# A two-layer hybrid block on one core: the last experts call split into two halves, the decoder taken tile by tile, and a planner's numbers set anew

## The reference

```python
x = x + local_attention(layernorm(x))     # "A": 16 heads, 44 fixed offsets (0..40, 96, 128, 384)
x = x + experts(layernorm(x))             # "F"
x = x + causal_attention(layernorm(x))    # "B": 16 heads, full causal softmax
x = x + experts(layernorm(x))             # "F" again, same weights

def experts(n):                                      # D=256, H=512, M=64, E=8
    cont   = sigmoid(n @ enc_W + enc_b) @ s2c_W + s2c_b          # 512 -> 64
    gates  = top2(softmax(tanh(cont @ rW1 + rb1) @ rW2 + rb2))   # renormalised
    h      = relu(cont @ We1[e] + be1[e])                        # 8 experts, 256 wide
    out    = sum_e gates[e] * (h[e] @ We2[e] + be2[e])
    spikes = sigmoid(out @ c2s_W + c2s_b)
    return layernorm(sigmoid(spikes @ dec_W + dec_b)) * ln_g + ln_b
```

## Time and profile before

| what | value |
|---|---|
| median of three timed runs | 1737.67 us (1734.58, 1737.67, 1738.28) |
| the profiled execution: its time | 1734.03 us |
| its span, first to last instruction | 1731.9 us |
| mean granted TensorE clock | 0.977 of full speed |
| busy: PE, DVE, ACT, POOL | 91%, 74%, 45%, 8% of the span |
| PE idle in front of a matmul, from 1655 us on | 14.2 us, in ten places |
| from the last decoder product to the end of the span | 11.5 us |

### The profile page before, as it was taken

The page is one execution under the profiler, slowest core; times in us unless marked ns, Lnnn a source line. Parts: engine busy times, 40 slices in busy tenths (PEclk is TensorE's granted clock), DMA queues, the critical chain, the costliest instruction groups (busy, mean ns, idle before and its releaser), DMA issues. The chain is left out here.

```text
span 1731.9 us, 28223 instructions
## 1 busy us (share of the span) xinstructions
PE 1580.9 (91%) x10560; PEld 882.0 (51%) x10560; DVE 1282.0 (74%) x3138; ACT 787.8 (45%) x1474; POOL 141.6 (8%) x155
## 2 busy tenths in 40 slices
PE   6599899999999999999999999999989998997976
PEld 2164465546555465554654556454655546454533
DVE  7969757896569966798767976699666996746633
ACT  1134346445364544644355353644536444552633
POOL 1010110101101020000101011010200001000000
PEclk9899999999999999999999999999999999998989
DMA  9230440014301161022500244001520216013000
GB/s 318 79 121 1 159 148 2 16 73 172 86 3 39 50 219 40 2 87 86 172 2 15 75 141 117 2 16 74 184 75 3 74 50 207 5 39 111 3 13 13
DMA packets 50261, 133.96 MB, mean 77 GB/s; under 512 B 6256, under 2 KB 22576, under 8 KB 45520
## 3 DMA queue, kind: packets, MB, share of 16 engines
q1 hardware_dynamic: 50128, 132.16, 23.3%
HBM read 80.99 MB, written 46.04 MB: 73 GB/s over the span
## 5 line engine op out<-in xcount | busy, mean ns | idle before, releaser
L1306 DVE TENSOR_TENSOR arena_AB<-qT,kT 128x2048 f32<-128x2048 f32 (+3 forms) x240 | 400.1, 1719 | 11.9 <-PE bank L1625 5.5
L1361 DVE CUSTOM_DVE_ANT_0 bank<-bank,causal_b 128x512 f32<-128x512 f32 (+3 forms) x512 | 234.1, 525 | 105.4 <-PE bank L1697 104.9
L1543 PE MATMUL bank<-arena_F,kept 128*128 128x512 f32 x512 | 235.6, 609 | 7.2 <-DVE arena_F L1451 4.8
L1625 PE MATMUL bank<-arena_AB,slot_w 128*32 128x512 f32 x1408 | 198.1, 612 | 32.6 <-DVE arena_AB L1306 31.4
L1135 ACT ACTIVATE arena_AB<-bank 128x512 f32<-128x512 f32 (+1 forms) x352 | 167.0, 585 | 70.2 <-PE bank L1713 69.8
L1168 ACT ACTIVATE arena_F<-bank,kept 128x512 f32<-128x512 f32 x256 | 159.0, 688 | 20.0 <-PE bank L1543 17.7
L1543 PEld LDWEIGHTS bank<-arena_F,kept 128*128 128x128 f32 x512 | 96.5, 195 | 124.7 <-issue 113.1
L1543 PE MATMUL bank<-cont_hi,by_cont 128*128 128x512 f32 (+1 forms) x272 | 115.9, 426 | 9.6 <-DVE arena_AB L1361 6.5
L1821 PE MATMUL bank<-kept,arena_F 128*128 128x256 f32 x512 | 117.0, 382 | 7.1 <-ACT arena_F L1185 6.6
L1543 PE MATMUL bank<-xnT,kept 128*128 128x512 f32 x256 | 120.0, 622 | 2.2 <-ACT xnT L1060 1.5
L1806 PE MATMUL bank<-arena_F,kept 128*64 128x512 f32 x512 | 120.5, 602 | 0.4 <-ACT arena_F L1181 0.2
(11 more groups left out here) (186 smaller groups left out, 2359.9 us busy)
## 6 DMA issues: line engine op xcount, KB each, us to landing
arena_AB<-band SPq DMA_DIRECT2D x32, 1344.0 KB, 6.6
arena_AB<-stacks SPq DMA_DIRECT2D x64, 384.0 KB
stacks<-arena_AB SPq DMA_DIRECT2D x48, 256.0 KB, 2.6
band<-arena_AB SPq DMA_DIRECT2D x32, 328.0 KB, 3.9
stacks<-xnT SPq DMA_DIRECT2D x32, 256.0 KB, 2.6
band<-kT SPq DMA_DIRECT2D x4, 1352.0 KB, 23.1
stacks<-xn SPq DMA_DIRECT2D x16, 256.0 KB, 3.0
kept<-kept_pack SPq DMA_DIRECT2D x1, 3765.0 KB, 18.8
```

Of the source, the lines that this page charges most:

```text
L1306: ins = nc.vector.tensor_tensor(prod[SET_AT[i]][:, col:col + c, :], qT[:, hf, :].unsqueeze(1).broadcast_to([P, c, T]), k, ALU.mult)
L1361: ins = nc.vector.tensor_tensor_reduce(out=s, in0=s, in1=causal[:, (TT - 1 - i) * P:T], scale=-1.0, scalar=BIG, op0=ALU.add, op1=ALU.min, ...
L1543: ins = nc.tensor.matmul(out(ps), w, x, start=n == 0, stop=n == len(pairs) - 1)
L1625: ins = nc.tensor.matmul(ps[HS * col:HS * (col + 1), :], slot_w[:, slot(n), :], prod[SET_AT[i]][:, col, :], start=r == 0, stop=False, skip ...
```

## The change

1. `calls()` replaces the last F call by two, stages `G` (tiles 0 and 1) and `H` (tiles 2 and 3). All code of an F call takes its tiles from `tiles_of(u)`, so that every product, read and copy of G and H has 256 columns in place of 512, and statistics and `close` run over two tiles. G waits for `pr` of tile 1 of the last attention call, H for `pr` of tile 3.
2. G and H have semaphores of their own. H has its own normalised rows, turned rows, `hid` ring and decoder output, in the part of memory that attention uses (`arena_AB`).
3. In all F calls, `dec` is four products of one tile each, a bank each, with one bias addition on DVE (`dec_b`, 256 columns) and one tanh each; the first step of the second statistics is `stat_2`, tile by tile.
4. In the planner: durations of a band's `write` and `read` by tile, `DEPTH` 1.55 to 1.95, and other offsets in `PULL` and `CALL_PULL`. These move steps in all calls.

```diff
+def tiles_of(u):
+    first = {"G": 0, "H": 2}.get(u.stage)
+    return range(TT) if first is None else range(first, first + 2)
@@ local_phases
-            p.put(("write", i), ("SP", 0.4, ("p", i, "ACT")), ("DMA", 2.6))
+            p.put(("write", i), ("SP", 0.4, ("p", i, "ACT")), ("DMA", (2.3, 2.3, 6.3, 5.0)[i]))
-                                        *([("pB", k - 2, 1, "PE")] if k >= 3 else [])), ("DMA", 7.0))
+                                        *([("pB", k - 2, 1, "PE")] if k >= 3 else [])), ("DMA", (6.6, 8.3, 6.0, 6.5)[k]))
@@ expert_phases
-    for n in range(TT // 2):
-        p.put(("dec", n), ("PE", 3.43, *[("c2s", m, "ACT") for m in range(KF)]), ("DVE", 0.61))
-        p.put(("tanh", n), ("ACT", 1.1, ("dec", n, "DVE")))
-    p.put("stats_2", ("DVE", 2.1, ("tanh", 0, "ACT"), ("tanh", 1, "ACT")))
+    for i in tiles:
+        p.put(("dec", i), ("PE", 1.72, *[("c2s", m, "ACT") for m in range(KF)]), ("DVE", 0.36))
+        p.put(("tanh", i), ("ACT", 0.5, ("dec", i, "DVE")))
+    for i in tiles:
+        p.put(("stat_2", i), ("DVE", 0.36, ("tanh", i, "ACT")))
+    p.put("stats_2", ("DVE", 0.6))
@@ calls
+    last = moe.pop()
+    moe.extend(Call(s, 0, last.batch, last.layer) for s in "GH")
@@ the tables, two lines of them
-TICK, DEPTH = 0.02, 1.55
+TICK, DEPTH = 0.02, 1.95
-    ("F", "PE"): {"turn": -620, "hid": 316, "eo": 1710, "dec": 10230},
+    ("F", "PE"): {"turn": 960, "rh": 479, "hid": 478, "eo": 2100, "dec": 9870},
@@ between_calls
-                needs.append((ATTENTION[n], ("pr", TT - 1), "DVE"))
+            needs.append((ATTENTION[min(n, len(ATTENTION) - 1)], ("pr", tiles_of(u)[-1]), "DVE"))
@@ build
+SIGNALS["G"] = SIGNALS["H"] = {**SIGNALS["F"], "xn_ready": 2, "dect_ready": 2}
+        hid_g = part(RH * T, at=STACKS).rearrange("p (r t) -> p r t", r=RH)
+        xn_g = part(TT * D, at=STACKS).rearrange("p (i c) -> p i c", i=TT)
+        xnT_g = part(KD * T).rearrange("p (k t) -> p k t", k=KD)
+        def rows_in(u):
+            return slice(tiles_of(u)[0], tiles_of(u)[-1] + 1)
+        def columns_in(u):
+            return slice(P * tiles_of(u)[0], P * (tiles_of(u)[-1] + 1))
@@ SP, experts
-                    sp.dma_start(rows_of(out_dram, u.batch), x_of[k][:]).then_inc(y_stored[k], 16)
+                    sp.dma_start(rows_of(out_dram, u.batch)[:, rows_in(u), :], x_of[k][:, rows_in(u), :]
+                                 ).then_inc(y_stored[k], 16)
@@ VectorE
-                    nc.vector.tensor_tensor(dd[:, 2 * p:2 * p + 2, :], ps[:].rearrange("p (i c) -> p i c", i=2),
-                                            c("dec_b").unsqueeze(1).broadcast_to([P, 2, D]), ALU.add
-                                            ).then_inc(read, 1)
+                    nc.vector.tensor_tensor(dd[:, p, :], ps[:, 0:D], c("dec_b"), ALU.add).then_inc(read, 1)
+                elif kind == "stat_2":
+                    dve.wait_ge(*nth(u, "dect_ready", p - tiles[0] + 1))
+                    tile_moments(u, dd, norm, p, "_2")
@@ TensorE
-                    product(u, name, lambda ps: ps[:], [(w, cont_hi), (w, cont_lo)])
+                    product(u, name, lambda ps: ps[:, 0:width], [(w, cont_hi[:, cols]), (w, cont_lo[:, cols])])
-                    for i in range(2):
-                        at = (2 * n + i) * P
-                        for k in range(KF):
-                            ins = nc.tensor.matmul(ps[:, i * D:(i + 1) * D], t_moe[:, k, at:at + P], dec_w[:, k, :],
+                    for k in range(KF):
+                        ins = nc.tensor.matmul(ps[:, 0:D], t_moe[:, k, n * P:(n + 1) * P], dec_w[:, k, :],
```

More of the change, by code:

```diff
@@ L125, in put, with norm_phases @@
             before = engine
-def norm_phases(p):
-    p.put("stats", ("DVE", 1.95))
+def norm_phases(p, tiles=TT):
+    p.put("stats", ("DVE", 0.6 + 0.34 * tiles))
     p.put("pow", ("POOL", 1.0, ("stats", "DVE")))
-    p.put("xn", ("DVE", 1.35, ("pow", "POOL")))
+    p.put("xn", ("DVE", 0.34 * tiles, ("pow", "POOL")))
     for k in range(KD):
-        p.put(("turn", k), ("PE", 0.44, ("xn", "DVE")), ("ACT", 0.48))
+        p.put(("turn", k), ("PE", 0.11 * tiles, ("xn", "DVE")), ("ACT", 0.16 + 0.08 * tiles))
 def output_phases(p, kind, i, on_needs, far):
@@ L305, in expert_phases @@
[L305 removed]
+        p.put(("c2s", m), ("PE", us(0.86, 0.0), ("eo", E // 2 - 1, "DVE")), ("ACT", us(0.6, 0.16)))
+    for i in tiles:
[4 more added lines that the diff above has]
+    p.put("stats_2", ("DVE", 0.6))
     p.put("pow_2", ("POOL", 1.0, ("stats_2", "DVE")))
[L307 removed]
@@ L308, in expert_phases @@
-    if layer == 1:
+    p.put("close", ("DVE", us(3.4, 0.2), ("pow_2", "POOL"), ("ln_b", "DVE")))
+    if u.layer == 1:
         p.put("store", ("SP", 0.4, ("close", "DVE")), ("DMA", 7.0))
@@ L1409, in gate_experts @@
+                link(u, nc.vector.tensor_tensor(same_, other, own, ALU.is_equal))
+                link(u, nc.vector.tensor_tensor(same_, same_, before, ALU.mult))
+                link(u, nc.vector.tensor_tensor(above_, above_, same_, ALU.add))
+                link(u, nc.vector.tensor_reduce(rank_, above_, AX, ALU.add))
+                link(u, nc.vector.tensor_scalar(rank_, rank_, 1.5, None, ALU.is_lt))
             def gate_experts(u):
+                rows, tiles = rows_in(u), len(tiles_of(u))
@@ L1471, in experts @@
                     link(u, ins)
-                    for i in range(TT):
+                    for i in tiles:
                         ins = nc.vector.scalar_tensor_tensor(
```

254 lines of the change are left out of this document (142 added, 112 removed), and 8 rows, old and new, of the table CALL_PULL.

## The result

The changed kernel takes 1730.23 us (median of five runs, 1728.38 to 1732.76), the kernel before 1737.67 (five runs beside it, 1734.58 to 1738.28): ratio 0.996, interval [0.9948, 0.9972]. It is faster, by 7.4 us or 0.4%; the forecast was 21.7. 1730 lies in the range of 1703 to 1733, near its slow end.

A forecast was written before the change was run, and what follows sets the result against it. PE, busy 91% of the span, was taken as the bound, its idle tenth all there is to win. 1734.03 - 12.8 (last call) - 1.7 (A1) - 2.7 (B6 into B7) - 1.5 (middle) = 1715.3, raised to 1716; range 1703 to 1733.

The forecast's parts named there:

- The band (place 3): Local attentions, third `pA`: less PE work covers tile 2's band read; 0.7 us lost in each of six calls, 4 lost.
- B7 beside the last but one experts call: Stretch from B6's last `pr` to B7's: other moves of `S`, `prod` and `hid` taken at nothing.
- The last call: Last experts call in halves G and H: entry, clock, inner waits and end, less the halves' cost; -12.8 us.
- Entry: Before G's `turn`: G needs only tiles 0 and 1, so PE's 5.61 us wait becomes 2.1; 3.5 gained.
- Clock: Behind the last call's entry: 3.9 us lost at granted clock 0.51, half of it regained; 1.9 gained.
- Inner waits: Last experts call: products of the other half fill five PE waits summing to 6.22 us; 5.8 gained.
- End: After PE's last product: chain to the last `close` 5.2 us against 8.0, plus 0.3 at the store.
- A1: Before A1's first `pA`: a decoder product moves behind tile 0's scores, so the band starts earlier; 1.7 us gained.
- B6 into B7: DVE does `on` 0 and 1 before most of B7's splits, ending PE's 3.01 us wait; 2.7 gained.
- End of a local attention (place 2): Behind B1 to B5's old-order waits of 0.89 and 1.33 us: new order gains 1.1 five times, 5.5.
- What would show it: Signs in the profile after, among them idle near 2 us before G's `turn` and near 1 at the third `pA`.
- The middle takes it all: Rival: end gains as forecast, new order loses 2 to 3 us per local attention; 1737, no difference; chance 0.08.

The follow-up runs named there:

- old_new_b6end_b7: old_new_b6end with F14 beside B7 also in the changed kernel's order, up to B7's `on`: 1721.41 us.
- old_order_halves: Order of the kernel before, decoder steps by tiles, up to B7's first `on`; from there the changed kernel's, with G and H: 1723.41 us, ratio 0.992.
- old_new_b6end: old_order_halves with B6's `on`, `oNT`, `pr` and B7's `lo` in the changed kernel's order: 1720.62 us, ratio 0.9903.

## Why the prediction was wrong

The forecast was for the profiled execution first, so its terms can be set against the marks of the two profiles, in us:

```
                                          before    after   change  forecast
start to the c2s beside A2                 405.6    405.7    +0.2    -1.7
from there to the c2s beside A7           1021.2   1026.0    +4.8    -2.2
from there to the last pr of B6            142.3    141.8    -0.5    -2.0
from there to the last pr of B7             95.7    102.3    +6.6     0
from there to the end of the span           67.1     53.8   -13.3   -12.8
```

- **The band (place 3): the step that failed.** It said "the read for tile 2 can start only after tile 0's `pA`", set PE's work from there against the landing, and took 0.7 us a call, 4 in all, since "part of it takes the place of small pauses after it". In the new order the read starts at the landing of its own write, 2.6 to 2.9 us later, since the scores now come later relative to `pA`. Measured are 3 us in each of six calls, 18 in place of 4: the waits for the band, 1.6 a call, took the place of no others (those of the stretch without them are 20.2 us, before 19.4), and the low clock behind them adds 1.1 a call. With the write ahead of one read 10.8 us of this came back. It could have been read ahead of time: the landing of that write in before, 5.8 to 8.4 us, set against the distance in the new order from its issue to the end of tile 0's `pA`, 5.2 to 5.6. A step whose place on its queue is unchanged moves all the same when what it waits for moves.
- **Luck in the same term.** The wait that it computed, 1.3 us at the median landing, is near the 1.6 measured, but by two errors. The cover it gave as 5.3 us was 7.6 to 8.1 in the six calls, and the read landed after 6.4 to 6.8. Had the read started with tile 0's `pA`, as I had it, there would have been no wait.
- **B7 beside the last but one experts call: put at nothing, 6.6 us in the profile.** "The moves of `S`, `prod` and `hid` otherwise I take at nothing" covers this stretch. Its order accounts for part: 4.3 us there on the old middle (old_new_b6end_b7), 3.0 of them given back behind. The eight profiles with this order and no fill in it have 102.3 us or more there, the six with the old one 98.5 or less; yet the median of that run moved by only 0.8, and how much stays in the time is open. Single executions of one kernel with the new middle lie up to 15 us apart.
- **The last call: right.** -12.8 forecast; -13.3 with the decoder by tiles (old_order_halves against before). Entry 3.5: idle 5.61 to 1.82, 3.8. Clock 1.9: 3.4 lost to 1.6, 1.8. Inner waits 5.8: 5.2. End 3.1: 2.65 on the chain and 0.8 at the store, 3.4. The four make 14.2, so the halves cost about 0.9 for 1.5. The pairs of 256 columns start 0.12 us apart, so two of them cost what one of 512 did; the doubt that a weight load might not hide is gone.
- **A1: the wait came out, the gain did not.** PE's idle time before the first band went from 5.74 to 4.10, 1.6 for 1.7. But that `pA` starts at 202.40 against 202.56, and the `c2s` beside A2 comes 0.2 us later with 0.8 us less work before it.
- **B6 into B7: right.** 2.8 for 2.7, by old_new_b6end.
- **End of a local attention (place 2): too small.** 5.5 forecast. In the five turns the second stretch, without `tS` 3, lost 15.8 us and the whole 4.8, so the rest gained 11.0, part of it by other moves. What can be named is the clock, which falls behind A2 in before and does not in after. Over these five stretches low clock is 3.4 to 8.5 us in all eight profiles with the old order of the middle and 0 in all eight with the new one. The forecast had counted B0's pattern against B1's over a whole turn, where this gain and the band's loss are mixed. No run isolates this place.
- **The signs.** Nearly all that "What would show it" names came true, the wait near 1 us at the third `pA` among them, and the forecast was wrong all the same: a wait tells what it costs only together with what stands behind it.
- **The rivals.** "The middle takes it all" named the right place and the right size, 2 to 3 us a local attention; I gave it 0.08. It did not come to 1737 because the ends of the local attentions gained more than I thought.

## What to carry to other kernels

For each transfer list all it waits for, and after a reordering recompute each of these times, also those that were never late: the one that binds may change though the queue's order does not. A write to memory that is read back is worth sending ahead of a large read, if the read has slack. Work that covers a latency is conserved: when it moves to cover one, ask what it covered before. The price of a low clock is not a term of the place where it shows: unless all waits of the stretch are filled or removed, it can come back at the next. And a stretch between two marks that became shorter is a gain only if the same work lies in it: look at its waits and its clock first.

## What the runs showed of the hardware

- The same write of 328 KB in A3 landed after 8.0 us with two reads of 1344 KB ahead of it, the first issued 2.9 us before it; after 6.5 with the first issued 4.8 us before it; and after 4.6 with one read ahead. Over A2 to A7: 7.8 to 8.4, 5.8 to 8.4 and 4.4 to 5.4.
- TensorE kept 2.4 GHz through 5 us of transposes whose results nobody reads, and fell to 1.2 GHz behind the same 5.6 us spent waiting (1.00 against 0.66 in 1572 to 1580); at the band a wait of 1.10 us left it at 1.00, one of 1.91 did not, and of two nearly equal ones, 1.60 and 1.62, only the first was followed by the lower clock.
- float32r products started 0.23 us apart at 512 columns and 0.12 at 256, each with 128 columns of weights of its own, whose load hid in both. PE in G, after:

```profile
1693.17 0.28 PE L1609 MATMUL bank<-cont_lo,by_cont 128*128 128x256 f32 x1
1693.29 0.28 PE L1609 MATMUL bank<-cont_hi,by_cont 128*128 128x256 f32 x1
```
